# A four-layer Perceiver forward pass: the dense block's matrices asked for two stages ahead, additions moved into its loop or onto TensorE, and the first statistics taken as x arrives

## The reference

```python
h = _ln(x, ln_conv_g, ln_conv_b)
...                                    # grouped causal convolution over 4 taps
x = x + jnp.transpose(conv, (0, 2, 1))
h = _ln(x, ln_attn_g, ln_attn_b)
...                                    # q, k, v; running means over the sequence
x = x + pooled_k * v
h = _ln(x, ln_boom_g, ln_boom_b)
h = jax.nn.gelu(jnp.einsum('bsd,ed->bse', h, Wb) + bb, approximate=False)
h = jnp.einsum('bse,de->bsd', h, Wu) + bu
return x + h
```

## Time and profile before

| | us |
|---|---|
| median of 3 runs (lowest, highest) | 1993.25 (1987.1, 2001.68) |
| the profiled execution's own time | 2001.55 |
| its span, first to last instruction | 1999.7 |
| PE busy | 1621.9 (81% of the span) |
| DVE busy | 966.1 (48%) |
| ACT busy | 746.8 (37%) |
| POOL busy | 447.0 (22%) |

### The profile page before, as it was taken

One profiled execution on the slowest core, in us unless ns is written; L12 is line 12 of the kernel. 1 busy time (PEld: TensorE's weight loads), 2 busy tenths in 40 slices (PEclk: granted clock), 3 DMA queues, 4 the chain that ended last, 5 costly groups with the idle time before them and its releaser, 6 DMA issues. The chain is left out here.

```text
span 1999.7 us, 53705 instructions
## 1 busy us (share of the span) xinstructions
PE 1621.9 (81%) x22057; PEld 1388.6 (69%) x22057; DVE 966.1 (48%) x2112; ACT 746.8 (37%) x1700; POOL 447.0 (22%) x627
## 2 busy tenths in 40 slices
PE   6999846769995999785899679987599977878694
PEld 4888645659994777663788569985477956767674
DVE  5665373341116878626322446755746744344313
ACT  3555372124441555432233236652224323333122
POOL 3443102012212434210344222210102200010241
PEclk9999855679997999877899879998798989675698
DMA  3111000059973111001799633320101162000586
GB/s 133 51 51 35 5 1 3 4 202 325 329 278 107 50 51 45 6 3 67 233 317 316 222 141 102 94 60 3 45 26 43 31 232 91 4 2 7 176 303 205
DMA packets 81590, 219.98 MB, mean 110 GB/s; under 512 B 19112, under 2 KB 34984, under 8 KB 74096
## 3 DMA queue, kind: packets, MB, share of 16 engines
q1 hardware_dynamic: 73232, 194.78, 29.6%
q0 software_dynamic: 8160, 22.29, 3.0%
HBM read 201.62 MB, written 15.34 MB: 108 GB/s over the span
## 5 line engine op out<-in xcount | busy, mean ns | idle before, releaser
L2295 PEld LDWEIGHTS ps<-xt,w 128*128 128x128 f32 x1728 | 208.0, 196 | 37.9 <-issue 30.9
L2295 PE MATMUL ps<-xt,w 128*128 128x128 f32 x1728 | 216.3, 282 | 19.9 <-DMA w<-in_L_ffn_w 17.3
L2348 ACT ACTIVATE g<-ps,b 128x128 f32<-128x128 f32 x340 | 123.8, 367 | 248.5 <-PE ps L2295 199.9
L2305 PE MATMUL ps<-w,g 128*128 128x256 f32 x864 | 201.7, 381 | 0.3 <-DMA w<-in_L_ffn_w 0.2
L2305 PEld LDWEIGHTS ps<-w,g 128*128 128x128 f32 x864 | 158.4, 191 | 18.9 <-issue 0.8
L2386 POOL DMA_INDIRECT results<-y,dest x85 | 83.6, 984 | 259.3 <-DVE y L2514 259.3
L2381 POOL DMA_INDIRECT x<-rows,token x85 | 83.1, 978 | 261.5 <-DVEq L2481 236.5
L2506 DVE COPY xt<-ps 128x256 f32<-128x256 f32 x85 | 36.1, 424 | 208.2 <-PE ps L2285 190.4
L2514 DVE COPY y<-ps 128x256 f32<-128x256 f32 x85 | 36.1, 425 | 158.1 <-PE ps L2305 158.1
L754 PE MATMUL ps<-c,w 128*128 128x258 f32 x512 | 96.8, 301 | 8.7 <-DVE pt L1061 6.3
L390 PE MATMUL ps<-consts_sb,z_sb 128*128 128x128 f32 x176 | 39.2, 410 | 72.9 <-DVE z_sb L584 72.9
(11 more groups left out here) (446 smaller groups left out, 3630.8 us busy)
## 6 DMA issues: line engine op xcount, KB each, us to landing
w<-in_L_ffn_w SPq DMA_DIRECT2D x124, 512.0 KB
w<-in_L_ffn_w SPq DMA_DIRECT2D x46, 1024.0 KB
c<-in_ctx SPq DMA_DIRECT2D x96, 258.0 KB, 2.8
rows<-in_w_L_xattn SPq DMA_DIRECT2D x32, 192.0 KB, 2.5
rows<-in_w_L_xattn SPq DMA_DIRECT2D x8, 768.0 KB
c<-in_w_L_xattn SPq DMA_DIRECT2D x8, 514.0 KB
back<-results SPq DMA_DIRECT2D x16, 256.0 KB, 5.3
raw<-in_L_ffn_w SPq DMA_DIRECT2D x16, 256.0 KB, 2.7
```

The source lines that it names most:

```text
L2295: mm = nc.tensor.matmul(hidden_bank(par, h), b.w1[:, par, c, h * P:(h + 1) * P], b.xt[:, par, c, :], start=c == 0, stop=c == DC - 1)
L2305: mm = nc.tensor.matmul(k.ps[:, YB + par, 0:D], b.g[:, par, h, :], b.w2[:, par, h, :], start=h == 0, stop=h == HC - 1)
L2348: nc.scalar.activation(b.g[:, par, h, :], hidden_bank(par, h), func, bias=b.b1[:, par, h:h + 1]).then_inc(s.g_ready, 1)
```

## The change

Six edits:

- `load_inputs` asks for x in four pieces of two tiles, each with its own semaphore. DVE takes the statistics of each pair when it is there; ACT calls Sqrt once, when the constants are there. `prepare` of `L0_xattn` is called with `known=True`.
- The scaling into `k.z` moves from the first `prepare` of `L2_attn` into `convolve`, where ACT does it ahead of its copies; the two small DVE operations that make its factor move behind all eight norms.
- w1 and w2 of the dense block are asked for in the second `prepare` (`ahead`), which does not wait for them; the third has no loads. ACT waits for them in the dense block.
- In the dense block the two additions to x stand inside the loop over hidden units, behind the splits of units 3 and 5.
- In the mixtures with biases TensorE multiplies each tile of x with the identity into the bank that then takes the bias product; DVE's first sum of a tile reads that bank in place of x, and the two additions L2519 are gone.
- A buffer for the factor and a semaphore for the matrices are kept outside the stages.

```diff
-    with stage(k, "loaded") as (block, s):
+    with stage(k, "x_loaded0 x_loaded1 x_loaded2 x_loaded3 consts_loaded noted") as (block, s):
+        x_loaded = [s.x_loaded0, s.x_loaded1, s.x_loaded2, s.x_loaded3]
+
         @block.sync
         def _(sp):
-            sp.dma_start(k.x[:], k.in_x).then_inc(s.loaded, 16)
-            sp.dma_start(k.consts[:], k.in_const).then_inc(s.loaded, 16)
+            for pair in range(NT // 2):
+                sp.dma_start(k.x[:, 2 * pair:2 * pair + 2, :], k.in_x[:, 2 * pair:2 * pair + 2, :]).then_inc(x_loaded[pair], 16)
+            sp.dma_start(k.consts[:], k.in_const).then_inc(s.consts_loaded, 16)
             fetch_weights(k, sp)
-            sp.wait_ge(s.loaded, 32)
+            sp.wait_ge(s.consts_loaded, 16)
+
+        @block.scalar
+        def _(act):
+            act.wait_ge(s.consts_loaded, 16)
+            nc.scalar.activation(k.warm[:], k.eps[:, 0:1], ACT.Sqrt)
+
+        @block.vector
+        def _(dve):
+            for t in range(NT):
+                dve.wait_ge(x_loaded[t // 2], 16)
+                nc.vector.bn_stats(k.stats[:, t, :], k.x[:, t, :]).then_inc(s.noted, 1)
+            for t in range(NT):
+                dve.wait_ge(s.noted, t + 1)
+                nc.vector.bn_aggr(k.mv[:, t, :], k.stats[:, t, :])
 
...
-                for t in range(half * HT, (half + 1) * HT):
-                    act.wait_ge(s.norm_done, t + 1)
-                    nc.scalar.activation(once[:, t, :], z[:, t, :], ACT.Copy, scale=b.std2[:, t:t + 1]).then_inc(s.once_done, 1)
 
             def take_turned(half):
...
                 deviation(0)
-            if once is not None:
-                normed_once(0)
             take_turned(0)
             deviation(1)
-            if once is not None:
-                normed_once(1)
             if known and units:
                 take_turned(1)
...
                 dve.wait_ge(s.first_rstd, 1)
-                nc.vector.tensor_tensor(b.std2[:], b.std[:], b.rstd1[:], ALU.mult).then_inc(s.std2_ready, 1)
+                nc.vector.tensor_tensor(k.std2[:], b.std[:], b.rstd1[:], ALU.mult)
 
             if not known:
                 statistics(0)
             norm(0)
-            if once is not None:
-                deviation_after()
             if known:
                 norm(1)
             else:
                 statistics(1)
             if w_at:
                 dve.wait_ge(*w_at)
+            if once:
+                deviation_after()
             if ws:
                 split(0)
...
             nc.scalar.copy(r.x[:, HI], k.ht[:]).then_inc(s.x_hi, 1)
+            if n_exp == 1:
+                act.wait_ge(k.raw_loaded, 32)
             round_w1(0, 0)
             round_w2(0, 0)
...
                         split(it, j, h)
+                        if also is not None and j == 0 and h == 3:
+                            nc.vector.tensor_tensor(into[:], into[:], also[:], ALU.add).then_inc(s.also_added, 1)
+                        if also is not None and j == 0 and h == 5:
+                            dve.wait_ge(s.also_added, 1)
+                            nc.vector.tensor_tensor(into[:], into[:], spread(row_bias, NT, 1), ALU.add).then_inc(s.bias_added, 1)
+                    if also is not None and j == 0:
+                        dve.wait_ge(s.bias_added, 1)
                     if not (last and j == UNITS - 1):
                         split(*ahead(it, j, 0, HC))
                     if last and j == UNITS - 1:
@@ -2156,15 +2172,10 @@
                 nc.vector.tensor_tensor(into[:], into[:], k.ps[:, 4:8, :].rearrange("p a (t d) -> p (a t) d", d=D),
                                         ALU.add).then_inc(s.bias_added, 1)
                 dve.wait_ge(s.bias_added, 1)
-            if also is not None:
-                nc.vector.tensor_tensor(into[:], into[:], also[:], ALU.add).then_inc(s.also_added, 1)
-                dve.wait_ge(s.also_added, 1)
-            if row_bias is not None:
-                dve.wait_ge(*w.at)
-                nc.vector.tensor_tensor(into[:], into[:], spread(row_bias, NT, 1), ALU.add).then_inc(s.bias_added, 1)
-                dve.wait_ge(s.bias_added, 1)
             dve.sem_inc(s.y_free, 4)
             split(0, 0, 0)
+            if also is not None:
+                dve.wait_ge(*w.at)
             if TURNS > 1:
                 with dve.Fori(0, TURNS - 1) as it:
...
                 for t in range(NT):
-                    mm = nc.tensor.matmul(k.ps[:, HB + t // 2, t % 2 * D:(t % 2 + 1) * D], turned.comb_t[0:W, t, :], w.b2[0:W, :],
-                                          start=True, stop=True)
-                    if t % 4 == 3:
-                        mm.then_inc(s.bias_done, 1)
+                    bank = k.ps[:, HB + t // 2, t % 2 * D:(t % 2 + 1) * D]
+                    nc.tensor.matmul(bank, k.ident, into[:, t, :], start=True, stop=False)
+                    nc.tensor.matmul(bank, turned.comb_t[0:W, t, :], w.b2[0:W, :], start=False, stop=True).then_inc(s.bias_done, 1)
 
             pe.wait_ge(s.idx_ready, 1)
...
 
-            def add_biases(half):
-                dve.wait_ge(s.bias_done, half + 1)
-                tiles = into[:, 4 * half:4 * half + 4, :].rearrange("p (h a) d -> p h (a d)", a=2)
-                nc.vector.tensor_tensor(tiles, tiles, k.ps[:, HB + 2 * half:HB + 2 * half + 2, :], ALU.add).then_inc(s.bias_added, 1)
-                dve.wait_ge(s.bias_added, half + 1)
...
             for pair in range(0, NT, 2):
-                if b1 is not None and pair % 4 == 0:
-                    add_biases(pair // 4)
+                if b1 is not None:
+                    dve.wait_ge(s.bias_done, pair + 2)
                 for n in range(top):
                     for t in (pair, pair + 1):
                         if n == 0:
                             dve.wait_ge(returned[t], 16)
                         else:
                             dve.wait_ge(s.summed, pair * top + 2 * n - 1 + t - pair)
-                        nc.vector.scalar_tensor_tensor(into[:, t, :], b.back[:, t, n, :], f.share[:, n, t:t + 1], into[:, t, :],
+                        sofar = into[:, t, :]
+                        if n == 0 and b1 is not None:
+                            sofar = k.ps[:, HB + t // 2, t % 2 * D:(t % 2 + 1) * D]
+                        nc.vector.scalar_tensor_tensor(into[:, t, :], b.back[:, t, n, :], f.share[:, n, t:t + 1], sofar,
...
 
-def convolve(k, w, hp, ct):
+def convolve(k, w, hp, ct, twice, once):
...
         def _(act):
+            for t in range(NT):
+                nc.scalar.activation(once[:, t, :], twice[:, t, :], ACT.Copy, scale=k.std2[:, t:t + 1])
             for q in (0, 2):
                 act.wait_ge(s.conv_done, q + 1)
...
                     cross_attention(k, w, b.qt, b, clamp=1.0e4 if name == "L1_xattn" else None)
             if name in ("L1_attn", "L3_attn", "L3_gqa"):
...
                     with buffers(k, hp=[P, DC, B, S + pad], ct=[P, DC, T]) as f:
-                        prepare(k, k.x, b.hn, padded=f.hp[:, :, :, pad:], gain=w.g1, shift=w.b1, w_at=w.at, known=True, once=k.z,
+                        prepare(k, k.x, b.hn, padded=f.hp[:, :, :, pad:], gain=w.g1, shift=w.b1, w_at=w.at, known=True, once=True,
                                 clear_early=[f.hp[:, c, :, 0:pad] for c in range(DC)])
-                        convolve(k, w, f.hp, f.ct)
+                        convolve(k, w, f.hp, f.ct, b.hn, k.z)
                         transpose_channels(k, f.ct, k.z, k.z)
-                    with buffers(k, q=[P, NT, 16, 17], key=[P, NT, 16, 17], v=[P, NT, 16, 17]) as f:
-                        prepare(k, k.z, b.hn, token_major=[(f.q, w.wq, w.bq), (f.key, w.wk, w.bk), (f.v, w.wv, w.bv)],
-                                gain=w.g2, shift=w.b2, w_at=w.at, known=True)
-                        pool_keys(k, f.q, f.key, f.v, k.z)
                     with buffers(k, raw1=[P, DC, 1024], raw2=[P, 1024 // P, D]) as raw:
                         w1, w2 = args["L2_boom_w1"], args["L2_boom_w2"]
-                        prepare(k, k.z, b.hn, ht=k.ht, gain=w.g3, shift=w.b3, w_at=w.at, known=True,
-                                early=[(raw.raw1[:], w1[0]), (raw.raw2[:], w2[0])])
+                        with buffers(k, q=[P, NT, 16, 17], key=[P, NT, 16, 17], v=[P, NT, 16, 17]) as f:
+                            prepare(k, k.z, b.hn, token_major=[(f.q, w.wq, w.bq), (f.key, w.wk, w.bk), (f.v, w.wv, w.bv)],
+                                    gain=w.g2, shift=w.b2, w_at=w.at, known=True,
+                                    ahead=[(raw.raw1[:], w1[0], k.raw_loaded), (raw.raw2[:], w2[0], k.raw_loaded)])
+                            pool_keys(k, f.q, f.key, f.v, k.z)
+                        prepare(k, k.z, b.hn, ht=k.ht, gain=w.g3, shift=w.b3, w_at=w.at, known=True)
                         w = begin("L2_boom")
                         ffn(k, w, 1, 1024, w1, w2, ACT.Gelu, None, None, k.x, b1=w.b1, row_bias=w.bo, also=k.z, raw=raw)
```

16 lines of the change are left out of this document (8 added, 8 removed).

## The result

| | before | changed |
|---|---|---|
| median (lowest to highest), 8 runs each | 1994.27 (1987.1 to 2001.68) | 1983.23 (1975.54 to 1991.75) |
| ratio, 95% interval | | 0.9939 [0.992, 0.9958] |
| the profiled execution, and its span | 2001.55, 1999.7 | 1982.8, 1980.9 |
| the same two kernels measured a second time, median | 1999.61 (23 runs) | 1980.4 (12 runs), ratio 0.9923 [0.9897, 0.995] |

The change makes the kernel 0.6% faster, 0.8% in the second measurement. 1983.23 lies inside the range (1963 to 1988), 7.9 us above the forecast: of 17.9 us promised, the ratios give 12.2 (8.4 to 16.0) and 15.4. Single steps are read better in the traces, stage by stage, since stretches that the change doesn't touch vary by several us from one execution to the next: between the last two square roots of the kernel before it is 83.9 us in one trace and 88.6 in the other.

The account below looks back on a forecast made before the run. TensorE was busy 81% of the span at mean clock 0.863; edits pay where a stage's end or TensorE waits. Terms 3.8 + 3.4 + 1.7 + 2.4 + 6.6 = 17.9 us off the 1993.25 median: 1975.3 us, range 1963 to 1988.

Parts of the forecast that it names:

- The start: Loading stage: statistics overlap x's arrival, so the first cross-attention's stage starts 6.6 us earlier; bounds 3.6 to 7.1.
- Matrices: Third prepare: asking for w1 and w2 earlier removes SP's wait, so the dense block starts 3.8 us earlier; bounds 3.0 to 3.8.
- Additions: Dense block: with both additions inside the loop at 2.29 us each, TensorE's first output product comes 3.4 us earlier.
- Scaling: First prepare of L2_attn: without the scaling, now run under the convolution, it is 1.7 us shorter; bounds 1.3 to 1.7.
- Rival B: Shorter TensorE gaps ahead of convolution and dense block let the clock give more back: 22 us gained, 1971 us; chance 0.20.
- Biases: Two mixtures: one bias addition of 1.21 us each leaves DVE's chain, 2.4 us together; bounds 0.8 to 2.4.
- A: Head of L0_xattn stays at the low clock, with late constants and weights: gain about 12 us, 1981 us; chance 0.20.
- C: Whole kernel slower because denser work lowers the mean granted clock, to 0.843: 2013 us; chance 0.03.
- D: The change does not do what it says; excluded from the order of instructions, given no chance.

Follow-up runs that it names:

- e1: The changed kernel with x asked for in one request, its statistics waiting for all of x: 1985.08 us, ratio 0.9928 [0.9901, 0.9954].
- e2: The changed kernel with x in four requests of 32 partitions each (8 KB rows), statistics waiting for all of x: 1981.03 us, one execution.
- e9: The changed kernel with x in two requests of four tiles, statistics waiting for their half: 1982.59 us, ratio 0.992 [0.9893, 0.9948].
- e8: The kernel before the change, unaltered, profiled once more: 2000.81 us.
- e4: The changed kernel with the dense matrices asked for in the third prepare again, but waited for by ACT in the dense block: 1983.55 us, one execution.
- e5: The changed kernel with the dense block's two additions back ahead of DVE's first split: 1983.19 us, one execution.
- e6: The changed kernel with the scaling back in the first prepare of L2_attn, between ACT's copies: 1986.05 us, one execution.
- e11: The changed kernel with extra ACT copies, later overwritten, that restore the old TensorE gap ahead of the convolution; scaling stays moved: 1986.38 us, one execution.
- e3: The changed kernel, unaltered, measured once more: 1980.4 us (12 executions), ratio 0.9923 [0.9897, 0.995] to the kernel before.

## Why the prediction held, and where it did not

**The start is the term that was mis-sized**: 6.6 forecast, 4.2 between the profiled executions, 4.5 between the means of two and nine traces (26.3 and 21.8), the lower half of its bounds. The step that failed is "Asked for in four pieces, x comes no later as a whole", and with it "The weights come at 9.9 or a little later": the landing times came from a trace in which x was one request, and e1, e2 and e9 show that all three loads land later when it is split. The prediction had the price of a request in hand ("half a microsecond apart") and charged nothing for the three more; being asked for later covers up to 1.4 of the 2.2 us, the slower transfer the rest. The square root came at 9.53, not 7.3; from there on the stage ran as said (12.5 us for 12.2, the products 6.23 for 5.75).

**Matrices: right in size, the reason too wide.** 3.7 us for 3.8 between the profiled executions, 2.9 against e8, whose third prepare was itself 0.8 shorter. No cost for what the transfer runs beside: the longer second prepare is there in e4 too, which has no transfer in it. e4 shows that the place of the wait earned the gain.

**Additions: right.** 3.4 us, as summed (e5 takes just this back), and each 2.28. The prediction's reading, that the 6.66 is a wait for POOL, is borne out by e5 against the loop: same addition, 6.66 beside POOL and 2.28 without. The Trainium skill, page "SBUF — State Buffer", section "Who interferes with whom", has the exclusion as a rule; 6.66 beside POOL's 5.28 and 2.28 without it agree. The pause's further price in clock was not in the sum.

**Scaling: 1.7 forecast, the stage's own 2.0 measured, but its neighbours moved more.** From the first square root to the third it is 70.35 us before, 70.46 in e8, 70.62 in e6 and 70.46 in e11, against 67.10 in the changed kernel and 69.11 in e3: 1.3 to 3.3 gained. Of the clock's share up to 2.8 is returned in the convolution and 1.5 taken in the second prepare. Rival B spoke of the first, and nothing in the prediction of the second.

**Biases: right.** 2.3 us for 2.4 between the profiled executions (1.44 + 0.89), 3.1 between the means of three traces with the additions on DVE (26.3) and eleven without (23.2). A sum out of PSUM takes 461 to 481 ns, out of SBUF 476 to 480: no price. TensorE's products were slower than I had them: with the eight more they took 10.0 us (599.93 to 609.94) in place of 7.4, at a granted clock of 1.00, and nobody waited.

**The sum.** Steps in the two profiled executions: 4.2 + 3.7 + 3.4 + 3.3 + 2.3 = 16.9 of the 18.8 by which they differ; the rest lies in untouched stages. With e3 it is 4.7 + 3.5 + 3.1 + 1.2 + 2.7 = 15.2. The second measurement's 15.4 us agrees; the first one's 12.2 is lower, with an interval up to 16.0, and what of this is chance was not settled. That 16.9 comes so near 17.9 is in part luck: the start gave 2.4 less than its term, and the clock, for which the sum had none, gave 1.3 in this pair of traces (2.8 less 1.5) and took 0.6 in e3 (0.9 less 1.5).

**The rivals.** A named 1981 us, nearer to the result than the forecast's 1975.3, and one of its reasons came true: late constants and weights. The one that it is named for did not: the products of L0_xattn's stage took 6.23 us, within 0.5 of the fast ones (5.7 to 6.7 in the nine traces). It rested on the clock's answer to transposes; there the changed kernel shows, in its third prepare, where TensorE had been idle for 7.21 us and had nothing but transposes since 1415.54:

```profile
1417.50:1418.50 1.00, 1.00 (x7) 1.00 (x6) 0.97 (x2) 0.78 (x1) 0.00 (x0) 0.50 0.00 0
1418.50:1419.50 1.00, 0.52 (x4) 0.28 (x2) 0.44 (x1) 0.44 (x1) 0.00 (x0) 0.91 0.00 0
```

The Trainium skill, page "TensorE: Matmul & The Clock Gate", section "Part 4: PE-mode transpose", says that transposes don't count as busy time for the clock in the way that other products do; here it rose within the second of these windows, behind 3 us of nothing else. C did not come: the mean clock is 0.868 for 0.863, not lower. D was excluded rightly.

## What to carry to other kernels

A wait at the end of a stage is paid by every engine; moved to the first instruction that reads the data, it may cost nothing, and how far ahead the data were asked for is a second question. When a load is split to start work sooner, don't take the landing times from the trace of the unsplit one: what follows in the queue is asked for later (0.47 us for each further request here) and can come later by more than the overlap earns. And a shorter pause of TensorE can change the clock of what comes tens of microseconds later, so measure the following stages as well.
